# Four layers on one core: additions ahead of the low part, shares and logits in another order, attention turns issued in another order

## The chip, the cores and the metric

One Trainium2 chip, one of its cores. TensorE (PE) multiplies matrices, VectorE (DVE) and ScalarE (ACT) do elementwise work, GpSimd (POOL) and SyncE (SP) mostly start transfers; each engine works through its own program in order, and waits on semaphores that the others raise. The time is device microseconds of one launch, the median of several runs. Lower is better.

## The reference

Input x has 64 batches of 32 tokens of 256 values: T = 2048 tokens, D = 256. Each layer adds to x:

```python
x = x + L0_ffn(L0_cond(x))     # w = weights[conditions]; einsum('bct,bcd->bdt'), then
                               # silu(x W1') * (x W3'), fwht, W2'   (hidden 1024)
x = x + L1_ffn(L1_cond(x))     # linear + LoRA of the batch's adapter; 32 experts, top 4, inner 96
x = x + L2_ffn(L2_cond(x))     # attention over a paged cache, window 128, new k and v written first;
                               # then a FFN on the top 1/8 of the tokens
x = x + L3_ffn(L3_cond(x))     # linear + LoRA; 8 experts, top 2, inner 176, plus a shared FFN, inner 704:
# L3: out = einsum('teh,te->th', ye, combine) + sigmoid(x sg) * (silu(x g) * (x u)) @ down
```

## The kernel before

The tokens are worked through as NCH = 4 chunks of 512, each of TPC = 4 tiles of 128 tokens. The order of all work is written out by hand, one program for each engine. In fp32 products a tensor is split in a high and a low part; `dve_low` (L488) makes the low part of a hidden piece on DVE once ACT has made the high one.

Layer 0 runs per chunk over eight pieces m of its hidden width. While chunk tc is computed, DVE does layer 1's routing of chunk tc-1 between the pieces: `dve_best`, `dve_chosen`, `dve_slots` (L641, which ends with the row numbers slot_i, L657) at m = 4 to 6, and at m = 6, behind that piece's low part, `dve_share` (L602) and twice `dve_share_half` (L614), which writes the weights of the rows into `outrows` (mid). ACT copies the rows (`act_copies`, L573), and POOL sends the rows with `pool_send` (L820), eight sends for each half chunk, to sent_d in DRAM. Behind the last chunk (ACT from L1239, DVE from L1675) the routing of chunk 3 goes half by half: on ACT logits of two tiles, a copy, `act_share` (L600), a copy. The copies of tile 2 wait until the rows of earlier chunks from that half of the buffer are sent. `dve_ends` (L660) then gives the ends of the experts' regions; with them SP and ACT write filler rows (L951 with 18 and L1251 with 14 fills), then SP loads keys for masks (L955), and POOL gathers the first blocks of 128 rows (xblk, L1033, with `dve_firsts`). 95 expert blocks follow, each turned (L726), multiplied (L736, L746, L754) and sent back to back_d.

Layer 2's attention goes over NT = 16 groups g of BPT = 4 batches. For a group POOL gathers the old cache rows (`old_rows`) and the newly written ones (`new_rows`) into the group's quarter of a buffer of four, and then the rows are turned by transfers from SBUF to SBUF (`rows_of`): four by SP (h=0) and four by POOL (h=1, `turn_rows`), into kv2, a ring of KV2 entries. Group 0's are shared by SP and ACT (`FIRST`). PE waits for all of a group's turns (L2219). `next_rows(g)` waits for the turns of group g-4 and gathers old rows of g; `new_rows(g)` waits for the old ones of g; `turn_rows(g)` waits for the new ones of g. All POOL transfers are in one order: `turn_rows(1)` to `(3)`, `next_rows(4)`, `(5)`, then for g = 4 to 15: `new_rows(g)`, `turn_rows(g-1)` if g > 4, `next_rows(g+2)`; at last `turn_rows(15)`.

Layer 3's shared FFN has MS = 6 pieces for each chunk. Chunks 0 and 1 run before the expert blocks, 2 and 3 after. In the last one (c = 3) PE also combines the returned expert rows of chunk m-2 at m = 2 to 5 (`combine3`, L2409: 32 matmuls with the identity into PSUM banks 4 and 5), after the gate and up product of piece m and before the down product of an earlier one. `combine3(c)` waits for `merged` to count c. DVE's `merged(c)` (L1985) adds the combined chunk to xT.

Of the kernel before, what the change touches and what calls it, by code (L numbers as in the profile page):

```python
# [8 lines left out]
ACT = mybir.ActivationFunctionType  # L9
# [12 lines left out]
NCH = T // CH  # L22
TPC = CH // P
BPT, BPC = P // S, CH // S
# [150 lines left out]
def build(nc, a):  # L175
    (late_at, _), (first_at, _), (cast_at, _) = constants()
    with ExitStack() as ctx:
# [706 lines left out]
        def _(sp):  # L884
# [94 lines left out]
            for g in range(NT):  # L979
                t = g % TPC  # L980
                sp.wait_ge(s["gone%d" % t], got_new(g))
                if g >= KV2:
                    sp.wait_ge(s["o_ps"], O_CREDIT + BPT * (g - KV2 + 1))
                if g == 0:
                    for q, name in enumerate(FIRST):
                        sp.dma_start(*rows_of(0, 0, q)).then_inc(s[name], 16)
                    continue
                for q in range(BPT):
                    sp.dma_start(*rows_of(g, 0, q)).then_inc(s["into%d" % t], 16)  # L989
            sp.wait_ge(s["o_ps"], O_CREDIT + BPT * (NT - KV2 + 2))  # L990
            sp.dma_start(sgu, gu3[:, :, :, E3 * F3:N3]).then_inc(s["shared3"], 16)
# [39 lines left out]
        def _(pool):  # L1031
# [59 lines left out]
            def turn_rows(g):  # L1091
                t = g % TPC
                pool.wait_ge(s["gone%d" % t], got_new(g))
                if g >= KV2:
                    pool.wait_ge(s["o_ps"], O_CREDIT + BPT * (g - KV2 + 1))
                for q in range(BPT):
                    pool.dma_start(*rows_of(g, 1, q)).then_inc(s["gone%d" % t], 16)
# [39 lines left out]
            nc.gpsimd.memset(Qbd, 0.0).then_inc(s["qzero"], 1)  # L1137
            pool.wait_ge(s["qsb_ready"], NCH)
            pool.wait_ge(s["fint_sb"], 2)
            for g in range(1, TPC):  # L1140
                turn_rows(g)

            def next_rows(g):
                t = g % TPC
# [8 lines left out]
            next_rows(TPC)  # L1153
            next_rows(TPC + 1)
            for g in range(TPC, NT):
                new_rows(g)
                if g > TPC:
                    turn_rows(g - 1)
                if g + 2 < NT:
                    next_rows(g + 2)  # L1160
            turn_rows(NT - 1)
# [23 lines left out]
        def _(act):  # L1185
# [50 lines left out]
                        nc.scalar.activation(b1s[:, D:D + E1], ps[:, 4, KD * E1:(KD + 1) * E1], ACT.Copy)\  # L1236
                            .then_inc(s["fold_sb"], 1)
            nc.scalar.activation(warm[:, 0:1], C["ones"][:, 0:1], ACT.Exp)
            for h in range(2):  # L1239
                for t in (2 * h, 2 * h + 1):  # L1240
                    act_logits(act, NCH - 1, t)
                act_copies(act, NCH - 1, 2 * h)
                act_share(act, L1, NCH - 1 + h)
                act_copies(act, NCH - 1, 2 * h + 1)

            nc.scalar.activation(warm[:, 1:2], C["ones"][:, 0:1], ACT.Silu)
            act.wait_ge(s["tables"], AT_FILLS)
            act.wait_ge(s["fill_set"], 2)
            for e in FILLS[1]:
                r = act.value_load(L1.endrow_i[0:1, e:e + 1], min_val=e * SPAN1, max_val=e * SPAN1 + T)  # L1250
                act.dma_start(*fill_rows(r, e)).then_inc(s["filled"], 16)  # L1251

# [46 lines left out]
            act.wait_ge(s["gone0"], got_new(0))  # L1299
            for q, name in enumerate(FIRST):  # L1300
                act.dma_start(*rows_of(0, 1, q)).then_inc(s[name], 16)

            act.wait_ge(s["masked"], 1)

# [115 lines left out]
        def _(dve):  # L1420
# [181 lines left out]
            for tc in range(NCH):  # L1602
                for m in range(M0):
                    if m == 3 and tc >= 1:
                        dve_adapter(dve, tc - 1)
                    if m == 5 and tc + 1 < NCH:
                        dve_y(tc + 1)
                    if tc >= 1 and m in (4, 5):
                        for t in (2 * m - 8, 2 * m - 7):
                            dve_best(dve, ch, L1, tc - 1, t)  # L1610
                        if m == 5:
                            dve_chosen(dve, ch, L1, tc - 1)
                    if tc >= 1 and m == 6:
                        dve_slots(dve, ch, L1, tc - 1)
                    dve.wait_ge(s["silu_ready"], tc * M0 + (m + 1))
                    row = silu[:, (tc * M0 + m) % SLOTS, :]
                    nc.vector.tensor_tensor(row, row, ps[:, 2 + m % 2, :], ALU.mult)\  # L1617
                        .then_inc(s["hfull_ready"], 1)
                    if m == 1 and tc >= 1:
                        if tc == 1:  # L1620
                            dve.wait_ge(s["x"], 16)
                        dve_residual(dve, tc - 1, 0)
                    dve_low(dve, m, P, tc * M0, hidh, hidl0)
                    if tc >= 1 and m == 6:
                        dve.wait_ge(s["poolhigh"], 1)
                        dve_share(dve, ch, L1, tc - 1)
                        for h in range(2):
                            dve_share_half(dve, tc - 1, h)
                    if tc == 0 and m == 0:
                        down_low()  # L1630
                        widen(2)
                    if tc == 0 and m == 1:
                        widen(3)
                    if tc == 0 and m == 1:
                        masks_of_adapters()
                        window_slots()
                    if tc == 0 and m in (2, 3):
                        for i in (range(0, 4) if m == 2 else range(4, 8)):
                            window_blocks(i)
                    if tc == 0 and m == 4:  # L1640
                        for i in range(8, WB):
                            window_blocks(i)
                    if tc == 0 and m == 5:
                        segments()
                    if tc == 1 and m == 1:
                        row_info()
                    if tc == 1 and m == 2:
                        tokens_seen(0)
                    if tc == 1 and m == 3:
                        tokens_seen(1)  # L1650
                    if tc == 1 and m == 6:
                        writers_match(0, P)
                    if tc == 1 and m == 7:
                        writers_last(0, P)
                    if tc == 2 and m == 2:
                        writers_match(1, B)
                    if tc == 2 and m == 3:
                        writers_last(1, B)
                    if tc == 2 and m == 6:
                        windows_match()  # L1660
                    if tc == 2 and m == 7:
                        windows_segment()
                    if tc == 3 and m == 0:
                        windows_new()
                    if tc == 3 and m == 2:
                        token_rows()
# [6 lines left out]
            for h in range(2):  # L1673
                for t in (2 * h, 2 * h + 1):
                    dve_best(dve, ch, L1, NCH - 1, t)  # L1675
                dve_chosen(dve, ch, L1, NCH - 1 + h)
                dve_slots(dve, ch, L1, NCH - 1 + h)
                dve_share(dve, ch, L1, NCH - 1 + h)
                dve_share_half(dve, NCH - 1, h)
            dve_ends(dve, ch, L1)  # L1680
            dve_table(dve, L1, 6)
            dve_firsts(dve, ch, L1)
            dve.wait_ge(s["keys"], 16)
            keynum, keyless = (zm[:, j * WK:(j + 1) * WK] for j in range(2))
# [303 lines left out]
            def shared_steps(c):  # L1988
                step = NCH * M0 + c * MS
                for m, w in enumerate(pieces(FS)):  # L1990
                    row = silu[0:w, (step + m) % SLOTS, :]
                    dve.wait_ge(s["silu_ready"], step + m + 1)
                    nc.vector.tensor_tensor(row, row, ps[0:w, 2 + m % 2, :], ALU.mult).then_inc(s["hfull_ready"], 1)
                    dve_low(dve, m, w, step, hidh3, hidl)
                    if c == 0 and m == 0:
                        dve_ends(dve, ch, L3)
                    if c == 0 and m == 3:
                        split_rest(1)
                    if c == 0 and m == 3:
                        dve_table(dve, L3, 4)  # L2000
                    if c == NCH - 1 and 2 <= m:
                        merged(m - 2)
                dve.wait_ge(s["acc_ready"], 2 * NCH + c + 1)
                dve.wait_ge(s["wb_sb"], c + 1)
                for d in range(KD):
                    last = nc.vector.tensor_tensor(scaled[c % 2][:, d, :], ps[:, 6 + d, :], wide3, ALU.mult)
                last.then_inc(s["acc_used"], 1)
                dve.wait_ge(s["acc_used"], 3 * NCH + c + 1)
                for d in range(KD):
                    cols = xT[:, d, c * CH:(c + 1) * CH]  # L2010
                    last = nc.vector.tensor_tensor(cols, scaled[c % 2][:, d, :], cols, ALU.add)
                last.then_inc(s["summed"], 1)
# [526 lines left out]
```

## Time and profile before

| | us |
|---|---|
| median of 3 runs | 1026.86 (1026.68 to 1029.39) |
| profiled execution | 1032.85 |
| its span | 1031.0 |
| PE busy | 857.0 (83%) |
| DVE busy | 569.4 (55%) |
| POOL busy | 387.7 (38%) |
| ACT busy | 361.7 (35%) |
| mean granted PE clock | 0.917 |

The profile is of one execution; times in it start at the span's begin. The slices of the page cut the span in 40 parts of 25.8 us, with the busy share in tenths, and PEclk the granted clock in tenths. The chain of waits goes from the last instruction back to what released it.

### The profile page before, as it was taken

Reading aid. Unit: us, or ns where it says so; the run is one execution under the profiler, and the core shown is the slowest. Engines: PE = TensorE matmul, PEld = TensorE weight load, DVE = VectorE, ACT = ScalarE, POOL = GpSimd, SP = SyncE. Lnnn points to the kernel's source line nnn. Section 1 sums busy time; section 2 is a strip of 40 time slices with the busy share of each in tenths; the row PEclk is TensorE's granted clock in tenths of the full one; section 3 lists DMA queues with packets and bytes.
Section 4 is the critical chain, followed back from the end, with each engine's and each line's share of the span. In section 5 each row is a group of like instructions: output and inputs, shape, how many; then the busy total and the mean of one; then the engine's idle time right before and its main releaser. Section 6 shows DMA issues by size and latency. Waiting matters only on the chain.

```text
span 1031.0 us, 17331 instructions
## 1 busy us (share of the span) xinstructions
PE 857.0 (83%) x5173; PEld 663.0 (64%) x5173; DVE 569.4 (55%) x1670; ACT 361.7 (35%) x1001; POOL 387.7 (38%) x411
## 2 busy tenths in 40 slices
PE   2999998921999998687159789979997989999976
PEld 2787776710778887454147678769456757777765
DVE  5547887551567766176239688851364444443322
ACT  3334252420334443022138578712243232222210
POOL 7200627275456666543525444000066003343000
PEclk9999999975899999898559899996999989999998
DMA  9143104688455552752367677400423103333031
GB/s 350 39 164 82 63 22 124 260 236 233 154 168 157 151 161 65 265 191 67 97 131 158 157 148 146 117 1 1 144 92 135 32 16 101 103 97 107 7 105 58
DMA packets 67243, 126.47 MB, mean 123 GB/s; under 512 B 20004, under 2 KB 49085, under 8 KB 64515
## 3 DMA queue, kind: packets, MB, share of 16 engines
q1 hardware_dynamic: 45407, 74.42, 24.2%
q0 software_dynamic: 20960, 48.76, 17.0%
q10 hardware_dynamic: 788, 2.19, 1.0%
q8 instruction: 46, 0.75, 0.3%
q14 instruction: 42, 0.34, 0.1%
HBM read 87.39 MB, written 43.30 MB: 127 GB/s over the span
## 4 chain that ended last, share of the span: by engine, by line
PE 31%; DMA 8%; DVE 7%; ACT 2%; SPq 2%; issue 2%; POOL 0%; DVEq 0%; POOLq 0%; ACTq 0%
PE ps L458 9%; PE ps L736 5%; PE ps L754 3%; DMA big<-newblk,new_i 2%; DMA early<-newblk,new_i 2%; SPq L989 2%; PE ps L2409 2%; PE ps L2364 1%; PE ps L2261 1%; PE ps L2303 1%; DMA early<-early 1%; DMA early<-big 1%; DMA big<-big 1%; DVE work L1840 1%; DVE early L1846 1%
## 5 line engine op out<-in xcount | busy, mean ns | idle before, releaser
L820 POOL DMA_INDIRECT sent_d<-mid,slot_i x88 | 98.2, 1116 | 114.3 <-DVE mid L619 68.4
L811 POOL DMA_INDIRECT back_d<-early,mid x95 | 94.0, 990 | 59.7 <-issue 41.8
L754 PE MATMUL ps<-early 96*128 (+1 forms) x346 | 97.4, 382 | 0.0
L492 DVE TENSOR_TENSOR hidl<-work,hidh 128x512 fp32r<-128x512 f32 (+1 forms) x56 | 38.8, 693 | 97.8 <-ACT hidh L485 97.8
L765 ACT ACTIVATE early<-ps 128x256 f32<-128x256 f32 x134 | 51.2, 383 | 111.8 <-PE ps L726 111.2
L736 PE MATMUL ps<-big,early 128*128 x380 | 88.1, 356 | 1.0 <-ACT early L765 0.4
L782 DVE TENSOR_TENSOR early<-early,ps 128x96 f32<-128x96 f32 (+1 forms) x134 | 37.2, 279 | 92.8 <-ACT early L770 73.7
L498 ACT ACTIVATE work<-ps 128x512 f32<-128x512 f32 (+1 forms) x56 | 33.3, 595 | 146.1 <-PE ps L458 146.0
L811 POOL DMA_INDIRECT back_d<-big,mid x39 | 38.4, 984 | 110.6 <-DVE big L795 108.3
L726 PE MATMUL ps<-late,mid 128*128 128x128 f32 x268 | 53.1, 280 | 23.4 <-DMA mid<-sent_d,first_i 22.1
L736 PEld LDWEIGHTS ps<-big,early 128*128 128x128 f32 x380 | 61.0, 194 | 10.4 <-issue 4.8
L726 PEld LDWEIGHTS ps<-late,mid 128*128 128x128 f32 x268 | 38.3, 145 | 39.1 <-issue 21.8
L770 ACT ACTIVATE early<-ps 128x96 f32<-128x96 f32 (+1 forms) x134 | 36.2, 270 | 76.3 <-PE ps L736 76.3
L754 PEld LDWEIGHTS ps<-early 96*128 96x128 f32 (+1 forms) x346 | 55.5, 191 | 6.3 <-issue 0.6
L458 PE MATMUL ps<-yhigh,l_high 128*128 128x512 f32 x128 | 55.1, 431 | 4.6 <-DVE ylow L1596 3.1
L736 PE MATMUL ps<-early 128*128 x156 | 55.1, 478 | 3.6 <-ACT early L765 3.6
L1312 ACT ACTIVATE early<-ps,early 128x176 f32<-128x176 f32 x128 | 50.9, 407 | 16.5 <-DVE early L1850 16.5
L1846 DVE TENSOR_REDUCE early<-ps 128x2 f32<-128x352 f32 x64 | 33.3, 521 | 36.8 <-PE ps L2230 35.9
L2230 PE MATMUL ps<-early 128*128 128x176 f32 x256 | 53.5, 335 | 0.0
L485 ACT ACTIVATE hidh<-work 128x512 fp32r<-128x512 f32 (+1 forms) x56 | 35.1, 627 | 52.1 <-DVE work L1617 43.7
L458 PE MATMUL ps<-ylow,l_high 128*128 128x512 f32 x128 | 51.3, 401 | 0.0
L458 PE MATMUL ps<-yhigh,l_low 128*128 128x512 f32 x128 | 51.3, 400 | 0.0
(399 smaller groups left out, 2090.6 us busy)
## 6 DMA issues: line engine op xcount, KB each, us to landing
mid<-sent_d SPq DMA_DIRECT2D x124, 130.0 KB
big<-back_d SPq DMA_DIRECT2D x16, 512.0 KB
early<-back_d SPq DMA_DIRECT2D x16, 256.0 KB, 3.3
early<-in_w SPq DMA_DIRECT2D x3, 1024.0 KB, 13.1
big<-in_gate SPq DMA_DIRECT2D x1, 3072.0 KB, 11.1
big<-in_up SPq DMA_DIRECT2D x1, 3072.0 KB, 11.3
early<-in_gu SPq DMA_DIRECT2D x1, 2816.0 KB, 10.8
sent_d<-work SPq DMA_DIRECT2D x19, 130.0 KB, 3.6
```

Of the source, the lines that this page charges most:

```text
L458: last = nc.tensor.matmul(out, w, x, start=start and n == 0, stop=stop and n == 2)
L492: nc.vector.tensor_tensor(low[0:w, slot, :], silu[0:w, slot, :], high[slot][0:w, :], ALU.subtract).then_inc(s["hid_ready"], 1)
L726: last = nc.tensor.transpose(ps[:, b % 2, k * P:(k + 1) * P], xblk[b % XRING][:, k * P:(k + 1) * P], ident)
L736: last = nc.tensor.matmul(ps[:, 2 + j % 2, 0:2 * F].rearrange("p (g n) -> p g n", g=2), L.yTb[j % 2][:, k * P:(k + 1) * P], L.gu[:, :, k, ...
L754: last = nc.tensor.matmul(ps[:, 6 + j % 2, 0:D], L.hTb[j % 2][0:f1 - f0, h * P:(h + 1) * P], L.down[0:f1 - f0, h, bass.ds(owners[j] * D, D ...
L765: nc.scalar.activation(L.yTb[b % 2], ps[:, b % 2, 0:2 * P], ACT.Copy).then_inc(s["turn_sb"], 1)
L782: nc.vector.tensor_tensor(L.hb[j % 2], L.sgb[j % 2], ps[:, 2 + j % 2, F:2 * F], ALU.mult)\
L811: nc.gpsimd.indirect_dma_start(out=back_d, out_offset=bass.IndirectOffsetOnAxis(ap=xblk[b % XRING][:, D:D + 1].bitcast(I32), axis=0), in_= ...
L820: nc.gpsimd.indirect_dma_start(out=sent_d, out_offset=bass.IndirectOffsetOnAxis(ap=L.slot_i[:, i:i + 1], axis=0), in_=L.rows[c][:, t, n, : ...
L1312: last = nc.scalar.activation(Pex[:, n % 2, h, :], ps[:, 2 + n % 2, h * WK:(h + 1) * WK], ACT.Exp, bias=acol[:, 1, n % 2, h:h + 1], scale= ...
L1846: nc.vector.tensor_reduce(acol[:, 0, n % 2, :], ps[:, 2 + n % 2, 0:2 * WK].rearrange("p (h c) -> p h c", h=2), X, ALU.max)\
L2230: last = nc.tensor.matmul(ps[:, 2 + n % 2, h * WK:(h + 1) * WK], Qbd[:, (n // 2) % 2, n % 2, h * P:(h + 1) * P], KTs[:, n % 2, :], start=F ...
```

## The change

D: in the last shared step, `merged(m-2)` for m = 2, 3, 4 stands between the product and `dve_low` of piece m, and that of m = 5 stays behind `dve_low`.

A: in layer 0 the wait for POOL and the shares of chunk tc-1 stand right behind `dve_slots`, before the product of piece 6.

B: at the end of layer 0 ACT makes all logits before the copies of tiles 2 and 3; these come after its first two fills, with the warming of Silu. DVE writes the weights of the last half behind `dve_ends` and `dve_table`.

C: SP issues only two of the four turns (h=0) of group 1; ACT issues the other two behind its own of group 0. POOL waits for the h=0 turns of group 1 between `turn_rows(1)` and `turn_rows(2)`; `turn_rows(3)` moves into the loop, where `turn_rows(g-1)` now stands before `new_rows(g)`.

```diff
@@ sync, attention
-                for q in range(BPT):
+                for q in range(BPT // 2 if g == 1 else BPT):
                     sp.dma_start(*rows_of(g, 0, q)).then_inc(s["into%d" % t], 16)
@@ gpsimd, attention
-            for g in range(1, TPC):
-                turn_rows(g)
+            turn_rows(1)
+            pool.wait_ge(s["into1"], turned(1))
+            turn_rows(2)
...
             for g in range(TPC, NT):
+                turn_rows(g - 1)
                 new_rows(g)
-                if g > TPC:
-                    turn_rows(g - 1)
                 if g + 2 < NT:
                     next_rows(g + 2)
@@ scalar, end of layer 0
-            for h in range(2):
-                for t in (2 * h, 2 * h + 1):
-                    act_logits(act, NCH - 1, t)
-                act_copies(act, NCH - 1, 2 * h)
-                act_share(act, L1, NCH - 1 + h)
-                act_copies(act, NCH - 1, 2 * h + 1)
-
-            nc.scalar.activation(warm[:, 1:2], C["ones"][:, 0:1], ACT.Silu)
+            for t in (0, 1):
+                act_logits(act, NCH - 1, t)
+            act_copies(act, NCH - 1, 0)
+            act_share(act, L1, NCH - 1)
+            act_copies(act, NCH - 1, 1)
+            for t in (2, 3):
+                act_logits(act, NCH - 1, t)
+            act_share(act, L1, NCH)
             act.wait_ge(s["tables"], AT_FILLS)
             act.wait_ge(s["fill_set"], 2)
-            for e in FILLS[1]:
+            for n, e in enumerate(FILLS[1]):
+                if n == 2:
+                    act_copies(act, NCH - 1, 2)
+                    act_copies(act, NCH - 1, 3)
+                    nc.scalar.activation(warm[:, 1:2], C["ones"][:, 0:1], ACT.Silu)
@@ scalar, attention
             for q, name in enumerate(FIRST):
                 act.dma_start(*rows_of(0, 1, q)).then_inc(s[name], 16)
+            act.wait_ge(s["gone1"], got_new(1))
+            for q in range(BPT // 2, BPT):
+                act.dma_start(*rows_of(1, 0, q)).then_inc(s["into1"], 16)
@@ vector, layer 0
                     if tc >= 1 and m == 6:
                         dve_slots(dve, ch, L1, tc - 1)
+                        dve.wait_ge(s["poolhigh"], 1)
+                        dve_share(dve, ch, L1, tc - 1)
+                        for h in range(2):
+                            dve_share_half(dve, tc - 1, h)
...
                     dve_low(dve, m, P, tc * M0, hidh, hidl0)
-                    if tc >= 1 and m == 6:
-                        dve.wait_ge(s["poolhigh"], 1)
-                        dve_share(dve, ch, L1, tc - 1)
-                        for h in range(2):
-                            dve_share_half(dve, tc - 1, h)
@@ vector, end of layer 0
                 dve_share(dve, ch, L1, NCH - 1 + h)
-                dve_share_half(dve, NCH - 1, h)
+                if h == 0:
+                    dve_share_half(dve, NCH - 1, h)
             dve_ends(dve, ch, L1)
             dve_table(dve, L1, 6)
+            dve_share_half(dve, NCH - 1, 1)
             dve_firsts(dve, ch, L1)
@@ vector, layer 3's shared steps
                     nc.vector.tensor_tensor(row, row, ps[0:w, 2 + m % 2, :], ALU.mult).then_inc(s["hfull_ready"], 1)
+                    if c == NCH - 1 and 2 <= m < MS - 1:
+                        merged(m - 2)
                     dve_low(dve, m, w, step, hidh3, hidl)
...
-                    if c == NCH - 1 and 2 <= m:
+                    if c == NCH - 1 and m == MS - 1:
                         merged(m - 2)
```

## Rows read from the trace of the kernel before

**Rows 1.** The page's 40 slices: PE's busy tenths and the granted clock.
```profile
PE   2999998921999998687159789979997989999976
PEclk9999999975899999898559899996999989999998
```
**Rows 2.** Chain of waits, 950 to 1031: start us, us, what.
```profile
980.33 3.57 PE ps L2409 x32
...
988.03 0.60 ACT work L498
...
989.87 1.21 DVE xT L1985 x2
...
991.12 5.47 PE ps L2409 x32
...
1003.82 3.84 PE ps L2409 x32
...
1020.41 4.38 PE ps L458 x18
```
**Rows 3.** Timeline of POOL, 190 to 245: start, duration, ..., [idle before <-releaser].
```profile
198.99 1.02 POOL L820 DMA_INDIRECT sent_d<-mid,slot_i  x1 [19.70 <-DVE mid L619]
...
239.78 0.96 POOL L820 DMA_INDIRECT sent_d<-mid,slot_i  x1 [0.30 <-issue]
```
**Rows 4.** Timeline of PE, 240 to 265.
```profile
251.37 0.66 PE L726 MATMUL ps<-late,mid 128*128 128x128 f32 x2 [20.14 <-DMA mid<-sent_d,first_i]
...
260.62 0.45 PE L746 MATMUL ps<-late,early 128*96 128x128 f32 x1 [1.67 <-DVE early L782]
```
**Rows 5.** Timeline of DVE, 194 to 262.
```profile
194.57 0.17 DVE L657 CAST slot_i<-dest_f 128x16 int32<-128x16 f32 x1
...
197.94 0.25 DVE L619 TENSOR_TENSOR mid<-share,total 128x8 f32<-128x8 f32 x2
...
226.91 0.16 DVE L607 TENSOR_REDUCE total<-share 128x2 f32<-128x8 f32 x1 [7.24 <-ACT share L600]
...
259.89 0.17 DVE L1686 TENSOR_SCALAR kv_f<-kv_f 128x17 f32<-128x17 f32 x1 [23.80 <-DMA zm<-in_first]
```
**Rows 6.** Timeline of SP, 224 to 262.
```profile
228.71 27.57 SPq L951 DMA_DIRECT2D sent_d<-work  x18
```
**Rows 7.** Timeline of PE, 530 to 533 and 655 to 656: first matmuls of a step.
```profile
532.25 0.42 PE L2219 MATMUL ps<-late,early 96*128 96x96 f32 x1 [6.33 <-DMA early<-early]
...
655.13 0.30 PE L2219 MATMUL ps<-late,big 96*128 96x96 f32 x1
```
**Rows 8.** Timeline of DVE, 975 to 1031: the product of piece 2.
```profile
982.12 0.68 DVE L1993 TENSOR_TENSOR work<-work,ps 128x512 f32<-128x512 f32 x1
```
**Rows 9.** Windows: us, length, busy of PE, PEld, DVE, ACT, POOL, PEclk, DMA share, GB/s.
```profile
250.00:260.00 10.00, 5.33 (x14) 3.15 (x14) 0.11 (x1) 1.65 (x5) 6.96 (x8) 0.50 0.83 246
```
**Rows 10.** Timeline of POOL, 494 to 646: gathers (L1033) and turns (L1097).
```profile
499.69 1.01 POOL L1033 DMA_INDIRECT early<-newblk,new_i  x1 [4.58 <-issue]
...
541.47 0.98 POOL L1033 DMA_INDIRECT early<-newblk,new_i  x1 [3.24 <-DMA early<-in_cache,win_i]
...
549.88 2.45 POOL L1097 DMA_DIRECT2D big<-early  x4 [0.77 <-DMA early<-newblk,new_i]
...
606.82 2.48 POOL L1097 DMA_DIRECT2D big<-big  x4
616.73 1.03 POOL L1033 DMA_INDIRECT big<-in_cache,win_i  x1 [7.43 <-DMA big<-big]
...
633.70 1.03 POOL L1033 DMA_INDIRECT big<-newblk,new_i  x1 [3.77 <-issue]
```
**Rows 11.** Chain of waits, 497 to 640: start us, us, what.
```profile
534.38 9.34 DMA early<-newblk,new_i
...
589.10 10.62 DMA big<-newblk,new_i
```
**Rows 12.** Timeline of SP, 500 to 580: its first turns.
```profile
506.63 6.90 SPq L986 DMA_DIRECT2D early<-early  x4
```

## The prediction

> **What bounds the kernel now.** I read the page's slices first: PE is near nine tenths busy nearly everywhere, and three places stand out, the 9th and 10th slice (206 to 258 us, two and one tenth), the 20th and 21st (490 to 541, one and five tenths) and, less so, the end [rows 1]. The change touches exactly these. So the question is, in each, what PE waits for last.
>
> At the end, the chain of waits runs mainly through PE. From 980.33 on it repeats one walk three times: a combine of 32 matmuls with the identity, the 18 matmuls of a product group, silu on ACT and its high part, the low part on DVE, and then two additions of the combined chunk (1.21 us), before the next combine may write the same PSUM banks [rows 2]. PE is idle from 988.01 to 991.12, 3.1 us, and as long in the two later rounds.
>
> At the junction of layer 0 and the experts, POOL sends the rows of the last two chunks, 32 sends back to back, from 198.99 (it had idled 19.70 us until DVE's shares) to 240.7 [rows 3]; a block can be gathered only when all rows have landed. PE's first transposes start at 251.37 [rows 4]. Then comes a second wait: PE stands 1.67 us at 260.62 for L782, since DVE, which works in order, sat 23.80 us at L1686 for the keys [rows 5], which SP loads behind its 18 fills of 27.57 us [rows 6].
>
> In attention each group g of four batches needs an old-row gather, a new-row gather and eight turns (four by SP, four by POOL). Early on PE waits for turns, 6.33 us at 532.25; by the end it waits no more, and the last group starts at 655.13 [rows 7].
>
> **Part D, the last shared step.** DVE adds merged(0), (1), (2) before the low part of the same m. merged(0) would run behind the product that ends at 982.80 [rows 8], once the combine that it adds has ended at 983.90, so until 985.2; the low part waits for ACT until 989.2 in any case, so it is hidden. On PE the next combine no longer waits for silu, high, low and additions: it starts at 988.01 instead of 991.12. That is 3.1 us three times, 9.4. The combine behind such an idle time took 5.47 us, others 3.57 and 3.84 [rows 2], and PEclk is eight tenths in the last slice [rows 1]; two of them (991.12 and the last, 1014.95 to 1020.41) were slow. Walked without idle time from 988.01: 3.57, 4.1, 3.57, 4.2, 3.57, 4.4 end at 1011.4 against 1024.8 (1020.41 + 4.38) [rows 2]. I take -13.3 (bounds -9.4, the stalls alone, and -14). What PE waits for next is nothing new: the back rows of chunks 2 and 3 land in time.
>
> **Parts A and B, the junction.** A puts the shares of a chunk right behind slot_i, which ends at 194.74, where they now come at 197.94 (the last step of them) [rows 5]. The three steps before it take 0.3, so the share is there at 195.0 and POOL's first send of chunk 2 starts 2.9 us earlier; the 32 sends behind it are back to back [rows 3], so their end is 2.9 earlier, if the DMA engines keep up. The product of m=6 is 0.7 us later, but PE has idle time behind it before the junction. For chunks 0 and 1 nothing moves, since POOL idles before the next chunk anyway (the 19.70 are such). B puts the logits of tiles 2 and 3 before ACT's copies of them, which wait until earlier rows are sent. Today ACT makes the share of the second half only behind them, and DVE waits 7.24 us for it [rows 5]; the ends table and the fills behind it come these 7.2 us earlier. The keys land near 252.5 and not 259.8, DVE isn't late, and PE's 1.67 us go. POOL needs the second share only behind 8 + 8 + 8 sends, at 227, and gets it at 225. The clock granted in 250 to 260 is 0.50 [rows 9]; what PE gets done sooner at half clock also ends it sooner, which I estimate at 0.8. The sum is -2.9 - 1.7 - 0.8 = -5.4. Against it: the DMA engines are 0.83 busy even in that stretch [rows 9] and the fills now compete with the sends; if all of the 2.9 is lost, it is -2.5.
>
> **Part C, the attention turns.** Today new_rows(g) is issued before POOL waits for the landing of g-1, so gathers overlap. The 11 new gathers behind that of 534.38 reach to 633.70, 9.03 us apart [rows 10, 11]. Four turns cost POOL 2.45 us of issue [rows 10]. With the change turn_rows(g-1), which waits for the landing of g-1, stands before new_rows(g). Queued behind that wait are the new gather and the next old one; PE waits for the turns of both. So one cycle holds the landing of a new gather + four turns + 0.3 of issue, and nothing overlaps. The latency of a new gather, from issue to turns: 6.9 us for the first of all (499.69 to SP's 506.63, hardly anything in flight) [rows 10, 12], 8.41 (541.47 to 549.88) [rows 10], 9.34 and 10.62 as the chain shows it [rows 11]; the mean of those waited for is about 9.6. So the cycle lies between 9.7 and 12.4 (13.4 at the worst). I take 8.4 + 2.5 + 0.3 = 11.2: the same packets are then spread over 11.2 and not 9.0 us, so less is in flight, and the row of 8.41 is the nearest to that. The start: the first turns of g=1, throttled and shared with ACT, may land up to 6.33 us sooner (525.9 to 532.2) [rows 7]; behind them now lie turns of 2, two old gathers and turns of 3 (2.5 + 1.3 + 1.3 + 2.5 = 7.6), then new(4) with 9.34: it lands between 542.8 and 549.1, I take 545. Today it lands at 543.72 [rows 11], so the gain of g=1 is swallowed there. new(15) lands at 545 + 11 x 11.2 = 668.2, its turns 9.9 later (606.82 to 616.73, a batch of turns and the gather that waits for it) [rows 10], at 678.1, against 655.13, when PE starts the last group today [rows 7]: +23.0. PE's own step, 7.5 us a group, no longer binds. Bounds: cycle 9.7 from 542.8 gives +4.3, cycle 12.4 from 545 gives +36.2.
>
> One rule bears on the gather's latency. A batch of turns issued at 606.82 lets its waiter go only at 616.73 [rows 10], and a new gather will come 2.5 us behind such a batch on the same queue. The Trainium skill, "DMA: Bandwidth & Descriptors", section "Two DMAs through the same engine are not ordered", says that within one queue of one DMA engine descriptors start in order. By that rule the gather can't land much before the turns ahead of it, so not much below 9.9 - 2.5 = 7.4 us; no row here has a new gather right behind turns.
>
> **Sum.** -13.3 - 5.4 + 23.0 = +4.3. The profiled execution took 1032.85 us (span 1031.0), 6 us above the median of 1026.86; made against it the sum gives 1037.2 (span 1035.3). I put the difference on the median: 1031.2.
>
> **Rivals.** (1) The new gather is fast when little else is in flight: latency 6.9 to 7.7, cycle 9.7 to 10.5, attention +4 to +15, in all 1012.5 to 1023.5: faster. It decides by the cycle alone: the net is zero where 11 x cycle - 100.2 = 18.7, at 10.8. For it speaks 6.9 with empty queues, against it the later rows of 8.4 to 10.6. (2) Cycle 10.5 to 11.1: within 3 us of today. (3) The latency stays at its mean of 9.6: cycle 12.4, attention +36, 1044: slower still. (4) The change does what its shape suggests: fewer transfers in flight at first, g=1 starts 6.3 earlier, and the waits cost nothing later: attention -6.3, in all 1002. For it speaks the wait at 532.25, against it the wait for a landing in every cycle. (5) Fills take the sends' share: junction -2.5, 2.9 more on each case. (6) The earlier additions do nothing, as the combine would then wait for its back rows: D is 0, 1044; nothing in the chain names such a transfer.
>
> **Chances.** Slower by over 0.3% (3.1 us, about what a measurement of this kernel can tell from no change) has 0.48: the forecast and its neighbours 0.33, (3) 0.13, (6) 0.02; (5) lies within these. Within 0.3% is (2), 0.22. Faster has 0.30: (1) 0.26, (4) 0.04. The range reaches into (1) and (3), 1014 to 1042, since both signs hold much; the likeliest case alone has 1028 to 1036.
>
> **What would show it.** D: combines of about 3.6 us with no wait ahead of the later ones. A: first send of chunk 2 near 196. B: SP's fills start near 221, no 23.80 us for the keys on DVE. C: new gathers on POOL 11.2 us apart, and PE waiting 3 to 4 us for turns in each group up to the last. The forecast is wrong if they are 9 us apart, or if the last combine's end doesn't move by 9 against its step's start.

## The result

The changed kernel takes 1046.26 us in the median of 4 runs (1040.81 to 1049.01), the kernel before 1028.12 (1026.68 to 1033.15); the ratio is 1.0154 (95% interval 1.0124 to 1.0183). Measured again in more rounds it is 1.0174 (1.0150 to 1.0198). So by the two ratios it is slower by 16 to 18 us, where I had forecast slower by 4.3 us: the sign was right, the size was not, and 1046 lies above the range.

The profiled execution of the changed kernel took 1040.81 us, with a span of 1039.0, against 1032.85 and 1031.0 before. The profiled execution of before is near the slowest of its runs and that of after is the fastest of its own, so their difference of 8.0 is smaller than that of the medians. The page's slices of after, to be read against [rows 1]:

```profile
PE   2999998914999995865467767797998998999997
...
PEclk9999999966999998987696898987999999999999
```

The junction's hole (9th and 10th slice) is a little smaller, the end is full, and from the 22nd to the 26th slice PE is at six to seven tenths, where it had been at seven to nine.

**The last step.** The chain of waits of after, from 1001 on (start, us, what), against [rows 2]:

```profile
1001.72 3.57 PE ps L2419 x32
1005.29 4.10 PE ps L458 x18
1009.39 3.57 PE ps L2419 x32
1012.96 4.16 PE ps L458 x18
1017.12 3.57 PE ps L2419 x32
1020.69 4.16 PE ps L458 x18
1024.84 3.57 PE ps L2419 x32
1028.41 4.38 PE ps L458 x18
```

DVE and ACT have left the chain, every combine takes 3.57 us, and none waits. From the first combine's start to the last product's end it is 31.07 us; before it was 44.46: -13.4, forecast -13.3. The granted clock over the two combines of 5.47 us before was 0.69 and 0.68; over the four combines of 3.57 us it is 1.00 now.

**The junction.** The timelines of POOL, PE and DVE of after (start, duration, ..., idle before and its releaser), against [rows 3], [rows 4] and [rows 5]:

```profile
193.38 1.02 POOL L820 DMA_INDIRECT sent_d<-mid,slot_i  x1 [16.92 <-DVE mid L619]
...
234.61 0.96 POOL L820 DMA_INDIRECT sent_d<-mid,slot_i  x1 [0.30 <-issue]
241.85 1.00 POOL L1033 DMA_INDIRECT mid<-sent_d,first_i  x1 [6.28 <-DMA sent_d<-mid,slot_i]
```
```profile
244.90 0.66 PE L726 MATMUL ps<-late,mid 128*128 128x128 f32 x2 [23.70 <-DMA mid<-sent_d,first_i]
```

The first send is 5.6 us earlier (forecast 2.9), the last one 5.2, PE's first transposes 6.5. SP's fills start at 218.60 instead of 228.71 [rows 6], and PE's stall of 1.67 us behind the keys is gone. DVE still waits 22.50 us for the keys, not 23.80, but now the wait ends at 248.46 and PE stands behind it no more. By the first attention turns of SP the kernel is 10.2 us ahead (496.46 against 506.63 [rows 12]).

**The attention.** One cycle out of the timeline of POOL of after, against [rows 10]:

```profile
597.94 1.03 POOL L1033 DMA_INDIRECT big<-newblk,new_i  x1 [0.30 <-issue]
599.27 1.00 POOL L1033 DMA_INDIRECT early<-in_cache,win_i  x1 [0.30 <-PE ps L2262]
607.42 2.45 POOL L1097 DMA_DIRECT2D big<-big  x4 [7.15 <-DMA big<-newblk,new_i]
610.17 1.03 POOL L1033 DMA_INDIRECT big<-newblk,new_i  x1 [0.30 <-issue]
```

The new gather, the old gather, a wait of 7.15 us for the new one to land, four turns, and only then the next new gather, 12.23 us after the last. From new(4), issued at 527.48, to new(15) at 657.93 the pace is 11.86 us, where it was 9.03. new(4) lands 38.3 us after SP's first turns (534.72 less 496.46), before 37.1: I had 38.4. PE's last group starts at 675.42, 179.0 us after those turns; before it was 148.5:

```profile
657.93 7.76 DMA big<-newblk,new_i
...
665.71 0.72 SPq L989
...
666.47 2.17 SPq L989
...
668.69 1.75 SPq L989
...
670.49 4.89 DMA big<-big
```

These rows are the end of the chain of waits through that stage (pieces of "issue" under 0.1 us are left out): new(15) lands, SP issues the turns, they land, PE begins.

The sum of the profiled pair: -10.2 at the start of attention, +30.5 in it, -13.4 in the last step, and +1.1 in between, 8.0.

### The profile page after: what moved, and what is told of

Same layout as the page of the kernel before. It is cut to its first block, busy times and chain, and to the rows that moved or that the text cites. A ratio compares the mean times of both kernels' runs of the same rounds, so it can differ in the third digit from the quotient of the medians.

```text
span 1039.0 us, 17332 instructions
## 1 busy us (share of the span) xinstructions
PE 854.0 (82%) x5173; PEld 665.1 (64%) x5173; DVE 571.1 (55%) x1670; ACT 363.8 (35%) x1001; POOL 386.9 (37%) x411
## 4 chain that ended last, share of the span: by engine, by line
PE 30%; DMA 13%; DVE 2%; POOL 2%; issue 2%; ACT 2%; SPq 1%; DVEq 0%; POOLq 0%; ACTq 0%
PE ps L458 9%; DMA big<-newblk,new_i 5%; DMA early<-newblk,new_i 5%; PE ps L736 5%; PE ps L754 3%; PE ps L2374 1%; POOL big L1097 1%; PE ps L2271 1%; PE ps L2419 1%; PE ps L2313 1%; DMA early<-early 1%; DMA early<-big 1%; DMA early<-in_cache,win_i 1%; SPq L989 1%; PE ps L2375 1%
## 5 line engine op out<-in xcount | busy, mean ns | idle before, releaser
L811 POOL DMA_INDIRECT back_d<-big,mid x39 | 38.4, 984 | 110.5 <-DVE big L795 108.1
L2240 PE MATMUL ps<-early 128*128 128x176 f32 x256 | 56.7, 350 | 0.0
```

The lines of the kernel that those rows point to most:

```text
L811: nc.gpsimd.indirect_dma_start(out=back_d, out_offset=bass.IndirectOffsetOnAxis(ap=xblk[b % XRING][:, D:D + 1].bitcast(I32), axis=0), in_= ...
L2240: last = nc.tensor.matmul(ps[:, 2 + n % 2, h * WK:(h + 1) * WK], Qbd[:, (n // 2) % 2, n % 2, h * P:(h + 1) * P], KTs[:, n % 2, :], start=F ...
```

## The experiments

They ran on four chips. On two of them the kernel before takes 1029 and 1033 us, on the two others 1084; seven experiments ran on these, four on one and three on the other (marked "5% slower chip"). Every ratio is against the kernel before on the same chip. Times and positions inside a kernel are of one profile each. How far such numbers scatter can be seen where the code of a stage is the same: in the profile of the last step alone, whose attention is that of before, the attention stage takes 153.2 us, against 148.5 before.

### One part at a time

**All edits but the attention ones.** The changed kernel, with the attention edits taken back:

```diff
-            turn_rows(1)
-            pool.wait_ge(s["into1"], turned(1))
-            turn_rows(2)
+            for g in range(1, TPC):
+                turn_rows(g)
...
             for g in range(TPC, NT):
-                turn_rows(g - 1)
                 new_rows(g)
+                if g > TPC:
+                    turn_rows(g - 1)
```

> The junction, ends and last-step edits are in, the attention is as before. Theory 1 (the attention edit alone makes the kernel slower, the rest gains): the attention stage starts about 10 us earlier than before (SP's first turns near 496.5), takes as long as before (from those turns to PE's last group 148.5 us) and the last step is 13.3 us shorter: 1028 - 10 - 13 = 1005 us (1000 to 1009). Rival (part of the 10 us of the earlier start is lost again because the transfers collide): 1012 to 1018.

1010.97 us against 1032.86: ratio 0.9781 (0.9749 to 0.9812), -22.5 us. The attention starts at 500.24, which is 6.4 us earlier than before and not 10, and PE's last group follows after 145.9 us. It is the fastest version, together with the one that keeps the old order in the loop, below. The expected 1005 stood on before's 1028; the chip's own before was 1032.9.

**The attention edit alone.**

> Only the attention edit (throttle, sharing with ScalarE, turns before new rows). Theory 1: new gathers come 11.9 us apart instead of 9.0, from SP's first turns to PE's last group 180 us instead of 148.5: 1028 + 31 = 1059 us (1052 to 1063). Rival (the long cycle comes from the earlier start of the stage or other traffic of the changed kernel, not from the order): under 1045.

1064.15 us, ratio 1.0297 (1.0266 to 1.0328), +30.7 us. New gathers are 11.77 us apart and the stage takes 177.9 us, with the junction as it was. So the long cycle comes from the edit itself, and not from the earlier start. A stretch of its chain of waits shows what it is made of, the gather's landing, POOL's turns and some tenths of a us of issue (its pieces are left out):

```profile
595.36 9.17 DMA early<-newblk,new_i
...
604.82 1.63 POOL big L1097 x3
...
606.69 0.34 POOL big L1097
...
607.60 8.68 DMA big<-newblk,new_i
...
616.57 1.62 POOL big L1097 x3
...
618.40 0.37 POOL big L1097
...
619.33 8.95 DMA big<-newblk,new_i
```

**The last step alone** (the two hunks with `merged`).

> Only the additions ahead of the low part in the last shared step. Theory (three stalls of 3.1 us and two combines at half clock go): first combine to end 31.1 instead of 44.5 us, 1028 - 13.4 = 1015 us (1013 to 1018). Rival (the half clock comes from elsewhere and stays): 1019.

1018.26 us, ratio 0.9856 (0.9821 to 0.9892), -14.8 us (-11.1 to -18.5). The combines are all 3.57 us, from 982.68 to the last at 1005.80. The rival, a half clock that stays (1019, so -9 us), falls by these combines and by the interval: the two slow combines of 5.47 us go with the idle time before them. Before, three combines stood behind 3.1 us of idle time, and one of them took only 3.84 us at a granted clock of 1.00; the other five profiles that have these stalls show the same, two of three at 5.2 to 5.5 us and one at 3.84. Why one is spared isn't shown.

### Which line of the attention edit

**The changed kernel with the old order in the loop.** The throttle of group 1 and the sharing with ScalarE stay:

```diff
             for g in range(TPC, NT):
-                turn_rows(g - 1)
                 new_rows(g)
+                turn_rows(g - 1)
```

> The changed kernel, with the loop over groups 4 to 15 issuing new rows of g before the turns of g-1 again; the throttle and the sharing of the first turns stay. Theory 1 (the order alone makes the cycle long): new gathers about 9 us apart again, from SP's first turns to PE's last group 142 to 150 us, in all about 1005 us (998 to 1011). Rival (the throttled first turns are what costs): 1025 or more.

1011.32 us, ratio 0.9788 (0.9759 to 0.9817). Two lines exchanged give back all of the loss: the pace is 8.78 us, the stage 148.5. It can't be told from the version without any attention edit (0.9781), so the throttled and shared first turns make no difference that can be told (one of 5 us would be seen). In its timeline new(5) goes out at 534.50 before POOL waits for new(4), so two new gathers are in flight:

```profile
529.37 0.99 POOL L1033 DMA_INDIRECT early<-newblk,new_i  x1 [7.26 <-DMA early<-in_cache,win_i]
530.38 2.49 POOL L1097 DMA_DIRECT2D big<-big  x4
533.17 1.02 POOL L1033 DMA_INDIRECT big<-in_cache,win_i  x1 [0.30 <-issue]
534.50 0.99 POOL L1033 DMA_INDIRECT early<-newblk,new_i  x1 [0.30 <-issue]
538.17 2.45 POOL L1097 DMA_DIRECT2D big<-early  x4 [2.67 <-DMA early<-newblk,new_i]
```

POOL waits 2.67 us there; in the changed order it waits 5 to 7.5 us in nearly each cycle, and starts nothing in that time.

### Can another order beat the old one

Both on one 5% slower chip, with all edits but the attention ones as their base. The base itself was measured only on a regular chip (0.9781). What compares on the slower chips is the pace of the old order there: 8.8 to 9.2 us in four profiles, of the junction edits below.

**Turns behind the old rows.**

```diff
                 new_rows(g)
-                if g > TPC:
-                    turn_rows(g - 1)
                 if g + 2 < NT:
                     next_rows(g + 2)
+                if g > TPC:
+                    turn_rows(g - 1)
```

> All edits but the attention ones; in the loop POOL issues new rows of g, old rows of g+2, and only then the turns of g-1. Theory 1 (a cycle is set by which landing POOL waits for next: the old rows wait for turns of g-2): the turns of g-1 now stand behind that wait, so their landing is later, the pace of new gathers 9.5 to 10.5 us instead of 8.9, and 1015 to 1028 us. Rival (POOL's wait for the landing was the costly one): 8 us or less, under 1005 us.

Ratio 0.9992 (0.9957 to 1.0027), where the base has 0.9781 on the other chip; pace 10.30 us, stage 163.4 us. The pace shows the loss against 8.8 to 9.2 of the old order. Theory 1 had 9.5 to 10.5. `next_rows(g+2)` waits until the turns of g-2 have landed, about 10 us after their issue, and now it stands right between the turns of g-2 and those of g-1. A wait for a landing that was started one step earlier sets the pace again.

**All turns by SyncE**, so that GpSimd only gathers:

```diff
-        TURNED, LATER = 16 * BPT, 16 * BPT
+        TURNED, LATER = 32 * BPT, 0
...
                 for q in range(BPT):
-                    sp.dma_start(*rows_of(g, 0, q)).then_inc(s["into%d" % t], 16)
+                    for h in range(2):
+                        sp.dma_start(*rows_of(g, h, q)).then_inc(s["into%d" % t], 16)
```

> All edits but the attention ones; SyncE issues all eight turns of groups 1 to 15, so that GpSimd never waits for new rows. Theory 1: GpSimd's own waits and its 2.5 us of issue per group leave the loop, a loop of landing, turns and old rows stays: new gathers 8 to 9 us apart, 1000 to 1012 us. Rival (eight turns in one hardware queue land later, since SyncE's issue already took up to 3 us for one): 10 us or more apart, over 1025.

Ratio 1.0118 (1.0084 to 1.0153), pace 11.0 us. The profile has a span of 1107.8 us, where the median of the runs is 1098.0, so the pace may be somewhat shorter in the others. The rival holds: GpSimd is freed, and the kernel loses. SyncE's timeline shows where; it is never idle between groups, and sixteen turns (two groups) take it 19 to 25 us:

```profile
568.57 22.27 SPq L990 DMA_DIRECT2D big<-big  x16
590.88 24.73 SPq L990 DMA_DIRECT2D big<-early  x16
```

Whether this is its issue alone or a full queue that holds it up, the run doesn't tell.

### What a gather's landing is made of

The forecast took 8.4 us from the issue of a new gather to the turns; it is 9.0 in the mean (12 waits, 7.5 to 9.9) in the changed kernel, and 9.3 in its second profile, which is from the chip of the next three runs. These take away the bytes of one neighbour at a time, with the number of transfers unchanged. They leave out rows of the keys, so they are read for the cycle; each ran once.

```diff
             n = 6 if h == 0 else WB - 6
+            if g > TPC and h == 1:
+                n = 1
```

> The changed kernel, but from group 5 on each of GpSimd's turns moves one partition's rows instead of five (the rest of the keys is left out, so the time is read only for the pace). Theory 1 (a new gather lands late since it is queued behind the four turns issued just before it on the same queue): its latency falls from about 9.1 to 7 us and the pace from 11.9 to 10 us or less. Rival (the latency is the gather's own or comes from SyncE's turns): pace still 11 us or more.

Pace 10.76 us, latency 8.3 in the mean. The same with `h == 0`:

> The changed kernel, but from group 5 on each of SyncE's turns moves one partition's rows instead of six (the rest is left out). Theory 1 (own queue): latency of new gathers stays at 8.5 us or more and the pace at 11.3 or more. Rival (SyncE's turns, in flight beside the gather, take the DMA engines): latency 7.5 or less, pace 10.3 or less.

Pace 11.12 us, latency 8.2. And the old rows:

```diff
-                gather((early, big)[half][p0:p0 + BPT * WB, 0:ROW], a["cache"], win_i[0:BPT * WB, g:g + 1],
+                n = BPT * WB if g <= TPC + 1 else 4
+                gather((early, big)[half][p0:p0 + n, 0:ROW], a["cache"], win_i[0:n, g:g + 1],
```

> The changed kernel, but from group 6 on the gather of old rows takes 4 rows instead of 44 (the rest is left out). Theory 1: the old gather is issued behind the new one, so it costs the new one little: pace 11 to 11.9 us. Rival (both gathers share the engines while in flight, so half of the latency is the old one's): latency 7.5 or less, pace 10.3 or less.

Pace 11.51 us, latency 8.5. For the old rows theory 1 holds (pace 11 to 11.9); for the two kinds of turns the result lies between theory and rival. Each neighbour has a share: its bytes are worth 0.5 to 0.8 us of latency against the 9.0 of the first profile, 0.8 to 1.0 against the 9.3 on the same chip, and none is the whole cause. The three took 1028.2, 1029.9 and 1037.6 us, where the changed kernel has 1047.7 on that chip. One cycle each of GpSimd's turns short and of all three short, the second on a 5% slower chip:

```profile
595.89 1.03 POOL L1035 DMA_INDIRECT big<-newblk,new_i  x1 [0.30 <-issue]
597.24 1.00 POOL L1035 DMA_INDIRECT early<-in_cache,win_i  x1 [0.30 <-issue]
604.27 2.02 POOL L1099 DMA_DIRECT2D big<-big  x4 [6.03 <-DMA big<-newblk,new_i]
606.59 1.03 POOL L1035 DMA_INDIRECT big<-newblk,new_i  x1 [0.30 <-issue]
```
```profile
613.62 1.04 POOL L1035 DMA_INDIRECT early<-newblk,new_i  x1 [0.30 <-issue]
614.97 0.98 POOL L1035 DMA_INDIRECT big<-in_cache,win_i  x1 [0.31 <-issue]
620.46 2.11 POOL L1100 DMA_DIRECT2D big<-early  x4 [4.52 <-DMA early<-newblk,new_i]
622.87 1.04 POOL L1035 DMA_INDIRECT early<-newblk,new_i  x1 [0.30 <-issue]
```

> The changed kernel, with all turns from group 5 on of one partition's rows and old gathers from group 6 on of 4 rows (the rest of the keys is left out). Theory 1 (each neighbour adds 0.4 to 0.8 us, the rest is the new gather's own): latency 7 to 7.5, pace 10.0 to 10.4 us. Rival (what is left is caused by the number of transfers issued, not by their bytes): latency stays at 8 or more, pace 10.7 or more.

Latency 7.5 us in the mean, pace 9.88, 1066.0 us. With most of the neighbours' bytes gone, the DMA engines are 0.28 busy between 590 and 690, against 0.63 between 560 and 650 in the changed kernel, and 7.5 of its 9.0 to 9.3 us remain. The rival, 8 us or more from the number of transfers, falls; a smaller part by their number isn't excluded, since the number was never changed, and no run has the full transfers in this order on that chip. The first new gather of all, 6.9 us with hardly anything in flight, points the same way: most of the latency comes without the neighbours' bytes. The cycle is that, plus four turns, plus 0.3 us; even so it stays above the 8.8 to 9.2 us of the old order on the slower chips. Of what was tried, only the overlap of gathers brings the cycle back to 9.

**The changed kernel again.**

> The changed kernel once more, in more rounds, since the first measurement spread over 8 us. If the parts add (all but the turns -22.5, turns alone +30.7 us, on one chip): +8 us, a ratio of 1.008 to 1.012. If the attention edit costs more when the stage starts earlier: 1.015 or more.

1047.7 us, ratio 1.0174. The parts measured by themselves on one chip give -22.5 + 30.7 = +8.2 us, and together, on another chip, they are at +16 to +18. The ratio falls on the second side, 1.015 or more, but that doesn't show its reason. The pace is 12.15 us in this profile and the stage 182.0 us, against 177.9 with the attention edit alone, while the stage without it is 145.9 against 148.5. That would be 6.7 us of the difference; by the first profile of the changed kernel (179.0) it is 3.7, and two profiles with the same attention code lie 4.7 us apart. So whether the stage goes slower when it starts earlier, or the chip and the scatter make the difference, no run tells apart.

This profile is a better measure than the first, since it took 1048.8 us, near the median. Against the profile of before its span of 1046.9 is 15.9 us longer: -5.3 at the start of attention, +33.5 in it, -13.4 in the last step, and +1.1 in between.

### The junction, edit by edit

Both twice, once on each of the two 5% slower chips.

> Only the shares of layer 0's chunks ahead of the product of piece 6. Theory 1 (the move fills idle time of VectorE at three places, not only before the last sends): products of the chunks run 0.5 to 3 us earlier, the first send of chunk 2 is at 193 to 194 instead of 199, PE's first expert transposes about 246, in all 5 us less than before (1028). Rival (the two sends' end is all that counts, 2.9 us): first send at 196, 1030 us against 1033 before.

Ratio 0.9959 (0.9926 to 0.9992), first send at 192.88, first gather at 242.72.

> Only the shares ahead of the product of piece 6, on another chip. If it has the gain that the traces show at the sends (5 us earlier): 0.995 of before. If half of it is lost in the filler rows and the keys, which come no earlier: 0.9975.

0.9974 (0.9951 to 0.9998), first send at 193.53, first gather at 243.27.

> Only the order at the end of layer 0 (all logits before the later copies, the weights of the last half later). Theory 1: the sends end where they did (239.8), PE's first expert transposes stay near 251, and the keys no longer hold VectorE: 2 to 3 us less than before. Rival (filler rows now run beside the sends and slow them): sends land a few us later, no gain or a loss.

1.0031 (1.0000 to 1.0063), first send at 198.27, first gather at 248.22.

> Only the order at the end of layer 0, on another chip. If the keys' wait was the only gain: 0.998 of before. If fills and sends collide: 1.000 or more.

0.9981 (0.9951 to 1.0011), first send at 196.98, first gather at 246.97. The shares put first bring the sends forward, by 5.4 us on one chip and 3.5 on the other against the profile with the other edit alone, and gain 0.3 to 0.4 per cent there. The order at the end of the layer alone gains nothing that can be told. On a regular chip only both together have a number: 0.9781 against 0.9856 with the last step alone, or -7.8 us. On the slower chips SP's 18 fills take 38 to 40 us instead of 27, so what the keys' wait is worth there says little of the regular ones; how the 7.8 us split on a regular chip stays open.

## Why the prediction was right or wrong

**Part D: right.** -13.3 forecast, -13.4 in the profile, -14.8 by the ratio of the run with this edit alone. Both terms, three stalls and two combines at a lowered clock, are there.

**Parts A and B: the sign right, the size too small, by a step that was wrong.** I wrote that for chunks 0 and 1 nothing moves, since POOL idles there. POOL does; but the edit also takes 0.6 us of work out of a stretch in which DVE is behind, and at whose end PE waits for it. The timelines of DVE, before and after, around the products of pieces 6 and 7 of chunk 2:

```profile
148.84 0.69 DVE L1617 TENSOR_TENSOR work<-work,ps 128x512 f32<-128x512 f32 x1 [0.79 <-ACT work L498]
...
150.83 0.16 DVE L607 TENSOR_REDUCE total<-share 128x4 f32<-128x16 f32 x1
...
151.40 3.34 DVE L1567 TENSOR_TENSOR big<-big,blkw 44x3072 f32<-44x3072 f32 x1
154.78 0.69 DVE L1617 TENSOR_TENSOR work<-work,ps 128x512 f32<-128x512 f32 x1
```
```profile
148.38 0.69 DVE L1628 TENSOR_TENSOR work<-work,ps 128x512 f32<-128x512 f32 x1 [0.22 <-ACT work L498]
149.76 0.69 DVE L492 TENSOR_TENSOR hidl<-work,hidh 128x512 fp32r<-128x512 f32 x1 [0.70 <-ACT hidh L485]
150.37 3.34 DVE L1574 TENSOR_TENSOR big<-big,blkw 44x3072 f32<-44x3072 f32 x1
153.75 0.69 DVE L1628 TENSOR_TENSOR work<-work,ps 128x512 f32<-128x512 f32 x1
```

DVE had waited 0.79 us for silu ahead of product 6 and was late for product 7 without a wait; the shares now fill that idle time (0.22 remain), and product 7 comes 5.37 us behind product 6 instead of 5.94. PE collects these 0.57 us where the chunk ends and it waits for DVE, before and after:

```profile
168.14 0.50 PE L458 MATMUL ps<-hidh,l_downh 128*128 128x512 f32 x1 [3.71 <-DVE xT L504]
```
```profile
167.11 0.50 PE L458 MATMUL ps<-hidh,l_downh 128*128 128x512 f32 x1 [3.14 <-DVE xT L504]
```

The same happens in chunk 1 (5.83 for 6.38), and at piece 3 of chunk 3 another 1.5 us go (6.45 for 7.99), where DVE had stood 0.61 us for a transfer that now has landed by then, and 0.93 us for ACT. In sum layer 0's last products are 2.7 us earlier. With the 2.9 of the move itself that is the 5.6 seen at the first send. The 1.5 us at that transfer don't come each time: over the twelve profiles with this edit the first send is at 192.2 to 196.0 (mean 193.7), over the five without it at 197.0 to 199.0, so 4.7 us is the better number for the send. The gain at the fills (10.1 us earlier, forecast 7.2, nearly all of the difference being these 2.7) and the end of the keys' stall came as forecast. From PE's first transposes on, the profile shows -6.5, the start of the attention stage -10.2, and in the other profiles with these edits -5.3 to -7.9. The -7.8 of the ratio rests on more runs, though it is a difference of two ratios that are each known to 3 us; forecast was -5.4. The 0.8 us for the half clock is in no run by itself (the granted clock of 250 to 260 is 0.95 now, before 0.50).

**Part C: the mechanism right, the term mis-sized.** A wait for a landing in every cycle, no gather beside another, and the gain of group 1 swallowed: all of this is there. The start, forecast at +38.4 us and measured at 38.3, is partly luck. POOL's wait for group 1 ended 18.1 us after SP's first turns, sooner than the 19.3 to 25.6 of the forecast, its issues took 7.5 (forecast 7.6), then POOL waited 5.43 us for the old rows of group 4, which I had left out, and new(4) landed in 7.2 us and not 9.34. The last turns take 9.7 us to land, forecast 9.9. The failed term is the cycle, and in it the gather's latency of 8.4 us: 11.2 forecast, 11.86, 12.15 and (attention edit alone) 11.77 measured, with a latency of 9.0, 9.3 and 8.9. Over eleven cycles that is 7.3, 10.4 and 6.3 us too little. The step behind it was "the same packets are then spread over 11.2 and not 9.0 us, so less is in flight, and the row of 8.41 is the nearest to that". I took the second shortest of the rows waited for because the load would fall; the load did fall, from 0.71 in the kernel before to 0.61 and 0.63 (DMA share of 550 to 600 and 600 to 650), and the latency only from about 9.6 to 9.0 or 9.3. The experiments with short neighbours go with that: 7.5 us are left without most of their bytes. The mean of about 9.6 (the three rows shown give 9.5) would have given a cycle of 12.4, and +36 us; the truth lies between.

The rule that I weighed, of the Trainium skill, "DMA: Bandwidth & Descriptors", section "Two DMAs through the same engine are not ordered", speaks of the order in which descriptors start, and says that they are pipelined; the floor of about 7.4 us for a new gather behind four turns was my estimate from it and the rows. In the changed kernel no waited latency is below 7.5, which agrees, but the turns ahead are not the main reason: with GpSimd's turns cut to a fifth of their rows the latency was still 8.3.

**The sum.** Read from the second profile of the changed kernel, the miss is nearly all in the cycle: -5.3 to the start of attention (forecast -5.4), +33.5 in the stage (forecast +23.0; eleven cycles of 12.15 and not 11.2 us make 10.4), -13.4 in the last step (forecast -13.3), +1.1 in between. That is +15.9; the profile of before is 3.9 us above the median that goes with it, that of the changed kernel 1.1 above its own, and by the medians it is +18.7. By the parts measured alone, on another chip, the sum is smaller: -14.8 - 7.8 + 30.7 = +8.1. Against the forecast part C is 7.7 more there, the junction 2.4 and the last step 1.5 less. The remaining 8 to 10 us show up only when the edits are together, and the cause of that stays open. My case (3), cycle at 12.4 and 1044 us, was the nearest of all, with a cycle of 11.9 to 12.2 in the runs; it had only 0.13, and the range ended at 1042.

**The rivals.** (1), a quick gather, falls: pace 11.9, and 9.9 even with most of the neighbours' bytes gone (on a slower chip). (4), the change does what its shape suggests, falls: the waits cost, and with the old order in the loop, where the throttle and the sharing stay, these gain nothing that can be told. (5), fills in the sends' way, isn't seen on the regular chips: 32 sends take 41.2 us from first to last, before 40.8. (6) falls by the run of the last step alone.

## What to carry to other kernels

On an engine that works in order, a wait for a landing belongs behind the issue of the next transfer, not ahead of it: exchanging two lines cost 35 to 40 us here, eleven cycles of 11.9 to 12.2 instead of 8.8 us. When a chain becomes serial, take the mean latency of the transfers that were waited for, not a short one on the argument that load will fall: here 7.5 of 9.0 to 9.3 us were left when most of the load was gone. And before calling a move free "since the consumer idles", look whether the engine it leaves or enters is late for somebody else: filling 0.8 us of idle time on DVE gained 0.6 us at two chunks.

## What the runs showed of the hardware

- A gather of 44 rows by GpSimd has 7.5 us in the mean from issue to its waiter when few other bytes are in flight (DMA share 0.28, on a slower chip), and 9.0 to 9.3 at shares of 0.61 to 0.63. Taking away one neighbour's bytes is worth 0.5 to 1.0 us.
- Putting all eight turns of a group on SyncE's queue is slower than four on SyncE's and four on GpSimd's, even though GpSimd is spared 2.5 us of issue a group: 1.0118 of the kernel before and a pace of 11.0 us, where the turns shared have a pace of 8.8 to 9.2 us on such chips (and 0.9781 on a regular one).
- PE's combines of 32 matmuls took 5.2 to 5.5 us (granted clock 0.69 and 0.68 in the kernel before) only when they stood behind 3.1 us of idle time, and in six profiles two of three such did; the third took 3.84 (clock 1.00). Without the idle time all four took 3.57, in eleven profiles.
- Two of the four chips run the kernel before 5% slower (1084 against 1029 and 1033 us). The profiles taken there show it ahead of attention: SP's 18 fills take 38 to 40 us instead of 27, and SP's first turns start at 541 to 549 in the kernels with only one junction edit, against 505 to 507 in those without one on regular chips. What makes these chips slower isn't shown.
